# Two selective-scan stages of a four-layer kernel: squares and a result copy on ScalarE, skip term, step bias and residual as TensorE products, softplus and gate reading PSUM

## The chip, the cores and the metric

The kernel runs on one core of a Trainium2 chip. The metric is device time in microseconds (us). The kernel before took 7786.44 us, the median of three runs (7783.06 to 7791.43).

## The reference, cut to what matters

Four layers run one after the other, each `x = x + s * silu(g)`, where `s` comes from a sequence mixer and `g` from a second network, both on the layer-normed `x`. Batch 8, 512 positions, width 128, fp32. The mixers of layers 0 and 2 are selective scans (L0a and L2a in the names of the kernel); the change touches these two alone. Per batch one of them computes:

```python
u, res = split(norm(x) @ in_proj_w)      # 256 + 256 columns
u = silu(causal_conv(u, conv_w, 4 taps) + conv_b)
dt, B, C = split(u @ x_proj_w)           # 8, 16 and 16 columns
delta = softplus(dt @ dt_proj_w + dt_proj_b)
h_t = exp(delta_t * A) * h_{t-1} + (delta_t * u_t) * B_t   # 256 x 16 states
y_t = sum over states of h_t * C_t
y = (y + u * D) * silu(res)
out = y @ out_proj_w                     # layer 2: + norm(x)
```

Layer 0 normalises by the root of the mean square, layer 2 by mean and variance.

## The kernel before

`mamba_net` (line 2070) is called twice, with `center=False, residual=False` for L0a and `center=True, residual=True` for L2a. The 256 inner channels are two halves `d` of 128 partitions; the free dimension holds the 512 positions of a batch. There are 16 states `n`, so 32 pairs (n, d) a batch. For each pair GpSimd forms `dbu = du * B` (L2255), ScalarE the decay `da = exp(A * delta)` in one of four PSUM banks (L2339), VectorE the scan (L2387) and, for three pairs of four, the product `hc` with C (L2396); the fourth is GpSimd's (L2260). TensorE sums the states by adding identity times `hc` into `y_ps[:, d]` (L2475).

Each engine has its own program, and `sequences` writes its order out by hand: `both(b, par)` runs through the 16 states of batch b. The end of batch b-1 (`gated`, then `result`) stands behind state 0, `result` behind state 0 on TensorE and behind state 1 on the others, and pieces of batch b+1 (`front`: norm, turn, in, tap, silus, dbc, dt, log) stand behind the states that `after_state` names, per engine. On the queue of an engine everything waits for what stands ahead of it. The first and last batch are outside the loop; the loop's body has two batches.

What the change touches:

- L2365, L2367: VectorE squares `x` and sums the squares (L0a). L2360, L2363: its moments by bn_stats (L2a). `measured` releases GpSimd's reciprocal root (L2236 to L2242).
- L2290 to L2299: ScalarE copies the step product from PSUM to `v` with its bias, then Abs, Exp, Ln. L2372: VectorE adds `max(v, 0)`: this is softplus.
- L2400, L2404, `gated`: VectorE adds the skip term `u * D` to `y_ps` into `ty` (two instructions), then multiplies by the gate `zs` into `yz`.
- L2489: TensorE's output product writes bank 0 of `y_ps`. L2412 (L2a, adding `f`) and L2414 (L0a): VectorE reads it into `result`; `stored` then releases the store on SyncE and TensorE's first state sum of the next batch, which overwrites that bank.
- L2351: VectorE forms diagonal matrices from `cols` for the four taps; L2434 uses them as products.
- `ring`: two PSUM banks, taken in turn by turn, in, conv, gate, dbc and dt products. A product waits until the previous content of its bank is read.

## Time and profile before

| | us |
|---|---|
| median of three runs | 7786.44 |
| profiled execution | 7796.52 |
| its span | 7794.6 |
| L0a, about 28 to 613 | 585 |
| L2a, about 6240 to 6840 | 600 |

The span reaches from the first to the last instruction. In the rows, PE is TensorE's products and PEld its weight loads, DVE is VectorE, ACT ScalarE, POOL GpSimd. A product of fp32 operands is two PE records, so "x4" in a timeline is two products. `[3.12 <-DVE x L2414]` says that the engine stood idle 3.12 us before the row and that VectorE's instruction of line 2414 released it. PEclk is the granted clock, 1.00 for 2.4 GHz and 0.50 for 1.2 GHz.

### The profile page before, as it was taken

What the parts mean: (1) busy time and instruction counts of PE and PEld (TensorE: products, weight loads), DVE (VectorE), ACT (ScalarE), POOL (GpSimd) and SP (SyncE); (2) the same over time, 40 slices, a digit from 0 to 9 for tenths busy, and PEclk for the clock granted to TensorE, in tenths of its full rate; (3) what the DMA queues carried; (4) which work ended last, traced back from release to release, by engine and by line L of the source; (5) the groups of instructions that cost most, each with busy time, mean ns of one, the idle gap of its engine ahead of it and who ended that gap; (6) DMA issues with size and microseconds to landing.
All of it is one profiled execution on the core that took longest, in us unless ns stands there. A gap on an engine that the chain in (4) does not pass through costs nothing. (4 is left out here: it accounts for less than half of the span.)

```text
span 7794.6 us, 241834 instructions
## 1 busy us (share of the span) xinstructions
PE 6366.5 (82%) x93078; PEld 4343.4 (56%) x93078; DVE 5662.3 (73%) x11712; ACT 4278.5 (55%) x7973; POOL 4672.3 (60%) x3762
## 2 busy tenths in 40 slices
PE   5776999999999999999998599977888757734268
PEld 2333666666666666666665588874555423322256
DVE  6885888888887888888886477766777668853533
ACT  5553666666666666666665344436777655512012
POOL 5776777777777777777776254544444357723000
PEclk8888999999999999999999799999999978867579
DMA  3332112112112112112111200001110033333001
GB/s 116 123 135 57 50 47 66 47 51 64 48 51 60 51 47 63 50 50 61 50 51 39 70 6 6 6 20 27 23 31 23 17 134 126 132 121 87 10 14 33
DMA packets 344463, 440.90 MB, mean 57 GB/s; under 512 B 151976, under 2 KB 235648, under 8 KB 324416
## 3 DMA queue, kind: packets, MB, share of 16 engines
q1 hardware_dynamic: 335632, 405.19, 17.0%
q8 instruction: 759, 12.44, 0.7%
q10 hardware_dynamic: 1584, 15.21, 0.5%
q0 software_dynamic: 6144, 5.25, 0.4%
q14 instruction: 344, 2.82, 0.1%
HBM read 217.42 MB, written 42.14 MB: 33 GB/s over the span
## 5 line engine op out<-in xcount | busy, mean ns | idle before, releaser
L1110 PE MATMUL L0f_ring<-L0f_wqkv,L0f_hT 128*128 128x512 f32 x2324 | 1196.5, 624 | 20.5 <-issue 18.0
L849 POOL TENSOR_TENSOR L0f_qr<-L0f_qs,L0f_table 128x512 f32<-128x512 f32 x776 | 990.8, 1277 | 216.7 <-issue 115.1
L856 POOL TENSOR_TENSOR L0f_qr<-L0f_qr,L0f_m 128x512 f32<-128x512 f32 x776 | 989.3, 1275 | 138.0 <-issue 119.6
L862 POOL TENSOR_TENSOR L0f_qr<-L0f_qr,L0f_rn 128x1024 f32<-128x1024 f32 x388 | 752.0, 1959 | 422.3 <-DVE L0f_rn L1016 400.3
L890 ACT ACTIVATE L0f_qs<-L0f_ring 128x512 f32<-128x512 f32 x776 | 460.1, 593 | 625.0 <-PE L0f_ring L1110 618.1
L993 DVE TENSOR_TENSOR L0f_m<-L0f_ring,L0f_table 128x512 f32<-128x512 f32 x776 | 531.4, 685 | 46.2 <-ACT L0f_qs L890 14.5
L1001 DVE TENSOR_REDUCE L0f_ssq<-L0f_sq 128x8 f32<-128x512 f32 x776 | 528.1, 681 | 29.6 <-ACT L0f_sq L895 13.7
L1110 PEld LDWEIGHTS L0f_ring<-L0f_wqkv,L0f_hT 128*128 128x128 f32 x2324 | 382.1, 190 | 266.9 <-issue 210.5
L895 ACT ACTIVATE L0f_sq<-L0f_qs 128x512 f32<-128x512 f32 x776 | 492.0, 634 | 36.0 <-DVE L0f_ssq L1001 4.2
L1116 PEld LDWEIGHTS L0f_ring<-const_ident,L0f_qr 128*128 128x128 f32 x3088 | 361.8, 141 | 178.2 <-issue 170.5
L1116 PE MATMUL L0f_ring<-const_ident,L0f_qr 128*128 128x128 f32 x3088 | 428.2, 274 | 16.6 <-POOL L0f_qr L862 16.6
L1022 DVE TENSOR_REDUCE L0f_mx<-L0f_scores 128x8 f32<-128x512 f32 x384 | 265.6, 692 | 165.5 <-PE L0f_scores L1135 160.5
L1182 PE MATMUL L0f_ring<-L0f_wo,L0f_oT 128*128 128x128 f32 x3088 | 382.5, 277 | 2.9 <-issue 2.1
L2475 PE MATMUL L0a_y<-L0a_hc,const_ident 128*128 128x512 f32 x512 | 288.6, 698 | 108.3 <-DVE L0a_hc L2396 86.7
L1165 PEld LDWEIGHTS L0f_scores<-L0f_vmix,L0f_pT 64*32 64x32 f32 x18480 | 264.7, 105 | 190.8 <-issue 185.0
L1182 PEld LDWEIGHTS L0f_ring<-L0f_wo,L0f_oT 128*128 128x128 f32 x3088 | 362.2, 193 | 10.0 <-issue 3.6
L1135 PE MATMUL L0f_scores<-L0f_kT,L0f_qT 64*32 64x64 f32 x24576 | 337.3, 224 | 36.9 <-issue 36.9
L2475 PE MATMUL L2a_y<-L2a_hc,const_ident 128*128 128x512 f32 x512 | 283.5, 687 | 101.3 <-DVE L2a_hc L2396 85.1
L904 ACT ACTIVATE L0f_vb<-L0f_ring 128x512 f32<-128x512 f32 x386 | 230.5, 597 | 246.7 <-PE L0f_ring L1110 246.4
L2255 POOL TENSOR_TENSOR L0a_dbu<-L0a_du,L0a_bc_all 128x512 f32<-128x512 f32 x256 | 325.3, 1304 | 57.1 <-DVE L0a_du L2375 50.2
L2255 POOL TENSOR_TENSOR L2a_dbu<-L2a_du,L2a_bc_all 128x512 f32<-128x512 f32 x256 | 325.3, 1304 | 54.6 <-DVE L2a_du L2375 50.7
L1165 PE MATMUL L0f_scores<-L0f_vmix,L0f_pT 64*32 64x64 f32 x18480 | 324.2, 224 | 34.4 <-SPq L155 10.3
(533 smaller groups left out, 17157.9 us busy)
## 6 DMA issues: line engine op xcount, KB each, us to landing
L0f_vmix<-L0f_vb SPq DMA_DIRECT2D x768, 128.0 KB
L0a_bc_all<-L0a_bc_rows SPq DMA_DIRECT2D x32, 2048.0 KB, 11.2
L2a_bc_all<-L2a_bc_rows SPq DMA_DIRECT2D x32, 2048.0 KB, 11.0
L0f_vmix<-L0f_vb SPq DMA_DIRECT2D x672, 64.0 KB
L1f_vmix<-L1f_vb SPq DMA_DIRECT2D x96, 128.0 KB, 2.3
L0f_wqkv<-L_ffn_wqkv_dram SPq DMA_DIRECT2D x7, 1536.0 KB, 6.0
L2f_parts<-L2f_zero ACTq DMA_DIRECT2D x8, 1088.0 KB, 12.7
n_s<-mixer_out SPq DMA_DIRECT2D x32, 256.0 KB, 4.9
```

The source lines that it names most:

```text
L849: e.tensor_tensor(rotated, qs[:, q % QN], spread(cos, 1, 8), ALU.mult).then_inc(cosed.sem, 1)
L856: e.tensor_tensor(rotated, rotated, m2[:, q % SN], ALU.add).then_inc(added.sem, 1)
L862: e.tensor_tensor(rotated, rotated, spread(rn[:, tt, 2 * c:2 * c + 2], 3, DH), ALU.mult).then_inc(scaled.sem, 1)
L895: e.activation(sq[:, q % SN], qs[:, q % QN], ACT.Square).then_inc(squared.sem, 1)
L993: e.tensor_tensor(m2[:, q % SN].rearrange("p h (a d) -> p h a d", a=2), swapped, spread(sin, 1, 8).rearrange("p h (a d) -> p h a d", a=2), ...
L1001: e.tensor_reduce(ssq[:, tt % 2, slot(step)], sq[:, q % SN], AX.X, ALU.add).then_inc(summed.sem, 1)
L1110: e.matmul(bank[:], hT[:, buffer_of(it, step), tt * P:tt * P + P], wqkv[:, layer % 2, col:col + 512], start=True, stop=True).then_inc(full, 1)
L1116: a = e.transpose(bank[:, j * P:j * P + P], qr[:, tt % 2, 2 * c + "qk".index(what), 2 * j:2 * j + 2, :], g.ident[:])
L1165: a = e.matmul(o_ps[cols, s, h, j], pT[half, s, j, cols], values, start=True, stop=True)
L1182: a = e.matmul(bank[:, 0:C], oT[:, tt % 2, j, :], wo[:, j, :], start=j == 0, stop=j == pairs - 1)
L2255: e.tensor_tensor(dbu[:, s], du[:, par, d], bc_all[:, n // QN, 0, n % QN], ALU.mult).then_inc(dbu_ready.sem, 1)
L2475: e.matmul(y_ps[:, d], g.ident[:], hc[:, (2 * n + d) % 4], start=n == 0, stop=n == states - 1).then_inc(added.sem, 1)
```

## The change

The squares of L0a become a step `moment` on ScalarE, behind state 0, with an accumulator output; in L2a the moments stay on VectorE. The diagonals of the bias and of `D` join those of the taps (14 in place of 8). TensorE adds the bias as diagonal times ones ahead of each step product, the skip term as diagonal times `uc` ahead of state 0's sum, and in L2a the residual as identity times `f` ahead of the output product. ScalarE takes Abs straight from PSUM, VectorE's softplus and gate read PSUM; `v` and `ty` are gone. ScalarE copies the result, behind state 1. The diff, cut to its core:

```diff
         # gpsimd, ahead of zeroed
+            e.memset(ones[:], 1.0)
+            e.memset(mv[:, :, 0], 0.0)
         # scalar, front (moment=0)
+                if kind == "moment":
+                    if not center:
+                        for tt in range(TT):
+                            o = e.activation(sq[:, tt], g.f[...], ACT.Square,
+                                             scale=C ** -0.5, accum_out=mv[:, tt, 1:2])
+                        o.then_inc(measured.sem, 1)
+                    return
         # scalar, front dt
-                        e.activation(v[:, d], ring.at(step)[:], ACT.Identity,
-                                     bias=cols[:, d, taps + 1:taps + 2]).then_inc(ring.empty_of(step), 1)
-                    e.drain()
-                    e.activation(ln1[:], v[:], ACT.Abs)
+                        e.activation(ln1[:, d], ring.at(step)[:], ACT.Abs)
         # scalar, back
+                if kind == "result":
+                    e.wait_ge(*out_full(b, "o"))
+                    e.wait_ge(sent[par], (b - par) * 8 + 16)
+                    e.activation(result[:, par], y_ps[:, 0].rearrange("p (t c) -> p t c", t=TT), ACT.Copy).then_inc(stored.sem, 1)
         # vector
-                for k in range(taps):
+                for k in range(taps + 3):
                     e.tensor_scalar(taps_of[:, d, k], g.ident[:], cols[:, d, k:k + 1], None, ALU.mult)
-                        e.scalar_tensor_tensor(sq[:], x, 1.0 / C, x, ALU.mult, ALU.mult)
-                        e.drain()
-                        e.tensor_reduce(mv[:, :, 1], sq[:], AX.X, ALU.add)
-                        e.scalar_tensor_tensor(delta[:, par, d], v[:, d], 0.0, ln1[:, d], ALU.max, ALU.add)
+                        e.scalar_tensor_tensor(delta[:, par, d], ring.at(step)[:], 0.0, ln1[:, d], ALU.max,
+                                               ALU.add).then_inc(ring.empty_of(step), 1)
-                    for d in range(D2):
-                        e.scalar_tensor_tensor(ty[:, d], uc[:, par, d], cols[:, d, taps + 2:taps + 3], y_ps[:, d],
-                                               ALU.mult, ALU.add)
-                    e.drain()
-                    e.tensor_tensor(yz[:], ty[:], zs[:, par], ALU.mult).then_inc(yz_ready.sem, 1)
-                elif kind == "result":
...
+                    e.tensor_tensor(yz[:], y_ps[:], zs[:, par], ALU.mult).then_inc(yz_ready.sem, 1)
         # tensor: dt, state 0, result
+                        e.matmul(ring.at(step)[:], taps_of[:, d, taps + 1], ones[:], start=True, stop=False)
+                    if n == 0:
+                        e.matmul(y_ps[:, d], taps_of[:, d, taps + 2], uc[:, par, d], start=True, stop=False)
+                        if residual:
+                            e.matmul(y_ps[:, 0, tt * C:tt * C + C], g.ident[:], g.f[...], start=True, stop=False)
```

## Rows read from the trace of the kernel before

**Rows 1.** Busy time by stretch, the two scan stages: length, then each engine, PEclk, DMA share, GB/s

```profile
28.00:613.00 585.00, 429.07 (x928) 181.82 (x928) 476.06 (x537) 298.31 (x434) 417.59 (x359) 0.85 0.30 120
6240.00:6840.00 600.00, 423.95 (x928) 179.58 (x928) 489.54 (x665) 312.02 (x465) 430.69 (x387) 0.82 0.32 126
```

**Rows 2.** Timeline of VectorE, first stage: start, length, engine, line, operation

```profile
142.96 1.41 DVE L2400 SCALAR_TENSOR_TENSOR L0a_ty<-L0a_uc,L0a_cols,L0a_y 128x512 f32<-128x512 f32 x2 [0.45 <-PE L0a_y L2475]
...
144.44 1.23 DVE L2404 TENSOR_TENSOR L0a_yz<-L0a_ty,L0a_zs 128x1024 f32<-128x1024 f32 x1
...
145.58 1.76 DVE L2365 SCALAR_TENSOR_TENSOR L0a_sq<-f 128x512 f32 x1
...
148.36 2.35 DVE L2387 TENSOR_TENSOR_SCAN L0a_da<-L0a_da,L0a_dbu 128x512 f32<-128x512 f32 x2 [0.26 <-issue]
...
151.80 0.68 DVE L2414 COPY L0a_result<-L0a_y 128x512 f32<-128x512 f32 x1
...
184.61 2.35 DVE L2387 TENSOR_TENSOR_SCAN L0a_da<-L0a_da,L0a_dbu 128x512 f32<-128x512 f32 x2 [3.03 <-ACT L0a_da L2339]
```

**Rows 3.** Timeline of TensorE's products, first stage

```profile
145.72 3.78 PE L2489 MATMUL L0a_y<-L0a_w_out,L0a_yz 128*128 128x128 f32 x16 [2.80 <-DVE L0a_yz L2404]
...
152.62 8.28 PE L2475 MATMUL L0a_y<-L0a_hc,const_ident 128*128 128x512 f32 x12 [3.12 <-DVE L0a_result L2414]
...
178.34 1.88 PE L2475 MATMUL L0a_y<-L0a_hc,const_ident 128*128 128x512 f32 x4
...
180.06 1.88 PE L2442 MATMUL L0a_ring<-L0a_xnT,L0a_w_in 128*128 128x512 f32 x4
...
427.47 7.08 PE L2475 MATMUL L0a_y<-L0a_hc,const_ident 128*128 128x512 f32 x12 [3.12 <-DVE L0a_result L2414]
...
559.82 9.49 PE L2475 MATMUL L0a_y<-L0a_hc,const_ident 128*128 128x512 f32 x16 [0.87 <-DVE L0a_result L2414]
```

**Rows 4.** Busy time by stretch around the boundaries, for the granted clock (PEclk)

```profile
152.60:158.50 5.90, 5.88 (x7) 2.51 (x8) 5.38 (x6) 2.89 (x7) 2.15 (x3) 0.50 0.14 44
559.80:564.65 4.85, 4.83 (x6) 2.17 (x7) 4.80 (x5) 1.30 (x2) 0.99 (x1) 0.50 0.18 54
6786.69:6790.56 3.87, 3.87 (x5) 1.80 (x6) 3.82 (x4) 0.99 (x2) 0.04 (x1) 0.50 0.23 72
424.80:427.40 2.60, 0.00 (x0) 0.00 (x0) 2.60 (x5) 1.23 (x2) 2.46 (x3) 1.00 0.00 0
428.10:431.50 3.40, 3.40 (x6) 1.34 (x5) 3.40 (x5) 2.24 (x5) 0.72 (x1) 0.50 0.24 77
```

**Rows 5.** Timeline of ScalarE, first stage

```profile
151.32 1.30 ACT L2339 ACTIVATE L0a_da<-L0a_delta,L0a_decay 128x512 f32<-128x512 f32 x2 [7.48 <-DVE L0a_hc L2396]
...
181.12 0.60 ACT L2312 ACTIVATE L0a_zs<-L0a_ring 128x512 f32<-128x512 f32 x1 [1.88 <-PE L0a_ring L2442]
...
188.50 0.69 ACT L2290 ACTIVATE L0a_v<-L0a_ring,L0a_cols 128x512 f32<-128x512 f32 x1 [1.13 <-PE L0a_ring L2450]
...
191.31 1.06 ACT L2295 ACTIVATE L0a_ln<-L0a_ln 128x1024 f32<-128x1024 f32 x1
```

**Rows 6.** Timeline of VectorE and of TensorE at a boundary of the second stage

```profile
6447.10 1.41 DVE L2400 SCALAR_TENSOR_TENSOR L2a_ty<-L2a_uc,L2a_cols,L2a_y 128x512 f32<-128x512 f32 x2 [0.45 <-PE L2a_y L2475]
6455.57 7.31 PE L2475 MATMUL L2a_y<-L2a_hc,const_ident 128*128 128x512 f32 x12 [1.92 <-DVE L2a_result L2412]
```

**Rows 7.** Groups of instructions by line (busy us, mean ns)

```profile
L2372 DVE SCALAR_TENSOR_TENSOR L0a_delta<-L0a_v,L0a_ln 128x512 f32<-128x512 f32 x16 | 15.3, 996 | 30.5 <-ACT L0a_ln L2299 30.5
L2323 ACT ACTIVATE L0a_upad<-L0a_ring 128x512 f32<-128x512 f32 x16 | 9.4, 590 | 4.8 <-PE L0a_ring L2463 4.1
L1764 ACT ACTIVATE L1f_scores<-L1f_scores,L1f_nmx,L1f_rn 128x128 f32<-128x128 f32 x504 | 218.7, 437 | 31.2 <-DVE L1f_nmx L1870 30.1
L1764 ACT ACTIVATION_READ_ACCUMULATOR L1f_scores<-L1f_scores,L1f_nmx,L1f_rn 128x1 f32 x504 | 106.0, 210 | 0.0
```

**Rows 8.** Timeline of VectorE at the start of the first stage

```profile
38.93 1.46 DVE L2351 TENSOR_SCALAR L0a_taps_of<-const_ident,L0a_cols 128x128 f32<-128x128 f32 x7
```

More of the change, by code:

```diff
@@ L2086, in mamba_net, with after_state @@
     ND_DVE = [k for k in ND if k not in ND_POOL]
-    FRONT = ([("norm",), ("turn",)] + [("in", c) for c in range(D2)] + [("tap", i) for i in range(2 * D2)] +
+    FRONT = ([("moment",), ("norm",), ("turn",)] + [("in", c) for c in range(D2)] + [("tap", i) for i in range(2 * D2)] +
              [("silus",), ("dbc",), ("dt",), ("log",)])
-    def after_state(norm, turn, silus, dbc, dt, log):
-        place = {("norm",): norm, ("turn",): turn, ("silus",): silus, ("dbc",): dbc, ("dt",): dt, ("log",): log}
+    def after_state(moment, norm, turn, silus, dbc, dt, log):
+        place = {("moment",): moment, ("norm",): norm, ("turn",): turn, ("silus",): silus, ("dbc",): dbc, ("dt",): dt, ("log",): log}
         place.update({("in", c): turn + 1 for c in range(D2)})
@@ L2115, in mamba_net @@
         upad = r.sb("upad", [P, D2, taps - 1 + SEQ])
-        taps_of = r.sb("taps_of", [P, D2, taps, P])
+        taps_of = r.sb("taps_of", [P, D2, taps + 3, P])
+        ones = r.sb("ones", [P, SEQ])
         uc = r.sb("uc", [P, 2, D2, SEQ])
@@ L2261, in back @@
                                         ALU.mult).then_inc(hc_pool_ready.sem, 1)
-            sequences(e, front, back, after_state(norm=2, turn=3, silus=7, dbc=8, dt=11, log=11))
+            sequences(e, front, back, after_state(moment=0, norm=2, turn=3, silus=7, dbc=8, dt=11, log=11))
         @block.scalar
@@ L2340, in back @@
                                  scale=decay[:, d, n:n + 1]).then_inc(da_ready.sem, 1)
-            sequences(e, front, back, after_state(norm=3, turn=5, silus=10, dbc=11, dt=12, log=13))
+            sequences(e, front, back, after_state(moment=0, norm=3, turn=5, silus=10, dbc=11, dt=12, log=13))
         @block.vector
@@ L2363, in front @@
                             e.bn_aggr(mv[:, tt], stats[:, tt])
[L2364 to L2368 removed]
+                        e.drain().then_inc(measured.sem, 1)
                 elif kind == "dt":
@@ L2449, in front @@
                         e.wait_ge(*ring.free(b, step))
+                        e.matmul(ring.at(step)[:], taps_of[:, d, taps + 1], ones[:], start=True, stop=False)
                         e.matmul(ring.at(step)[:], w_dt[:, d * P:d * P + P], dbc[0:rank, par],
-                                 start=True, stop=True).then_inc(ring.full_of(step), 1)
+                                 start=False, stop=True).then_inc(ring.full_of(step), 1)
                     return
@@ L2474, in add @@
                         e.wait_ge(*stored(b, "s", 1))
-                    e.matmul(y_ps[:, d], g.ident[:], hc[:, (2 * n + d) % 4], start=n == 0, stop=n == states - 1).then_inc(added.sem, 1)
+                    if n == 0:
+                        e.matmul(y_ps[:, d], taps_of[:, d, taps + 2], uc[:, par, d], start=True, stop=False)
+                    e.matmul(y_ps[:, d], g.ident[:], hc[:, (2 * n + d) % 4], start=False, stop=n == states - 1).then_inc(added.sem, 1)
                 if kind == "state":
@@ L2487, in back @@
                     for tt in range(TT):
+                        if residual:
+                            e.matmul(y_ps[:, 0, tt * C:tt * C + C], g.ident[:],
+                                     g.f[:, bass.ds(b * TT + tt, 1), :].rearrange("p o c -> p (o c)"), start=True, stop=False)
                         for d in range(D2):
                             o = e.matmul(y_ps[:, 0, tt * C:tt * C + C], yz[:, d, tt * P:tt * P + P], w_out[:, d, :],
-                                         start=d == 0, stop=d == D2 - 1)
+                                         start=d == 0 and not residual, stop=d == D2 - 1)
                     o.then_inc(out_full.sem, 1)
-            sequences(e, front, back, after_state(norm=0, turn=3, silus=9, dbc=10, dt=11, log=11), gated=0, result=0)
+            sequences(e, front, back, after_state(moment=0, norm=0, turn=3, silus=9, dbc=10, dt=11, log=11), gated=0, result=0)
 def ttt_net(nc, g, name, w):
```

25 lines of the change are left out of this document (7 added, 18 removed).

## The prediction, made before the changed kernel ran

> **What bounds the kernel now.** I read the busy time by stretch first, to see how much of the kernel the change can reach. The two selective-scan stages take 585 and 600 us of 7794.6; in both VectorE is the busiest engine, at 476 of 585 and 490 of 600 us, with TensorE at 429 and 424 [rows 1]. Eight batches make some 68 us each. A share of 81% is no proof of a bound, so the second view is the timelines of the boundary between two batches, engine by engine.
>
> VectorE at a boundary [rows 2]: the skip term (two instructions from 142.96), the gate product at 144.44, squares and their sum for the next batch from 145.58, the scans of state 1 at 148.36, the copy of the old batch's result at 151.80. TensorE meanwhile [rows 3]: the output product runs 145.72 to 149.50, then the engine idles 3.12 us until VectorE has read the result, because the accumulator bank is the same; the state sums start again only at 152.62, 9.66 us after the skip term began. From there TensorE has no wait left: its rows follow each other back to back into the gate products at 180.06, two of those shown [rows 3]. The first gate product is what ScalarE waited for, 1.88 us before the first gate Silu at 181.12 [rows 5], and behind ScalarE's table load VectorE stands still 3.03 us for state 11 [rows 2]. So the path of a batch runs: VectorE through the boundary, then **TensorE from its restart to the gate products**, then ScalarE. VectorE's own scans are hidden in the middle part, with 3 us to spare.
>
> The third view is the granted clock [rows 4]. TensorE comes out of the boundary at 1.2 GHz (0.50) and stays there 5.9 us after the restart at 152.6. At the last boundary, where nothing but the result read lies in the gap (0.87 us idle before 559.82 [rows 3]), it stayed slow for 4.85 us in the first stage and 3.87 in the second. Once, at 424.8, the clock was up right behind the output product and fell again at 428.1, after an idle gap like those above. I price TensorE's path as restart plus half of the slow time: 9.66 + 2.95 = 12.6 us. At the two boundaries with the loop's branch it is 11.8 (restart 10.1 after the skip term, at 427.47 [rows 3], and 3.40 us slow [rows 4]); mean of the six, 12.3. In the second stage the restart is at 8.5 (6447.10 to 6455.57 [rows 6]) with 3.9 us slow, 10.4; its six boundaries lie between 10.3 and 11.8, mean 10.7.
>
> **The change, part by part** (times count from where the skip term begins now).
>
> *Skip term to TensorE, squares to ScalarE.* VectorE loses 1.48 (142.96 to 144.44) and, in the first stage alone, 2.78 (145.58 to 148.36). The gate product now reads PSUM beside SBUF; the nearest rows are the skip instructions themselves, 1.41 us for two of 512 columns with one PSUM operand [rows 2], against 996 ns each for the delta instructions with none [rows 7], so I leave it at 1.2 us. The output product starts at 1.3 in place of 2.8. ScalarE's four squares with accumulator cost 437 + 210 ns each, overlapping [rows 7], some 1.8 us or at most 2.6, between the decays of states 0 and 1. ScalarE idles 7.48 us in that stretch (before 151.32 [rows 5]), and state 1 is not scanned until after the gate product: cost nothing. Without that cover it would be 1.8 us a batch. The second stage keeps its moments on VectorE.
>
> *Result copy to ScalarE.* VectorE loses 0.60 a batch. This adds a wait: ScalarE now stands for the output product, and the decays of state 2 are queued behind it, with VectorE's scans behind them. Output product 1.3 to 5.1 (3.78 us slow [rows 3]), copy 0.59 as other ScalarE reads of PSUM [rows 7], to 5.9; decay of state 2 at 6.6. VectorE is ready at 4.7, so it stalls 1.9. What matters is that TensorE restarts at 6.0, 3.7 earlier.
>
> *Skip matmuls.* Two 128x512 products per batch right behind the restart. Two such products (four records) start 1.72 us apart at 2.4 GHz [rows 3], so +1.72, all on TensorE's path. Slow time after the restart: the idle gap is now about 0.9, as at the last boundaries (3.87 and 4.85), with none possible as at 424.8; between 0 and 6 I take 3, costing 1.5. Path: 6.0 + 1.7 + 1.5 = 9.2, against 12.3. **First stage: 3.1 x 6 = 18.7 us.** VectorE by its own rows would finish state 3 at about 13.4 in place of 16.9, so it does not undo this.
>
> *Residual on TensorE, second stage.* Eight records on top of 16: 5.7 us in place of 3.78 if slow throughout, about 5.1 if the clock rises inside. Restart 7.3 (7.9 if slow); slow time then taken as 0, bound 6. Path: 7.3 + 1.7 = 9.0 against 10.7. **Second stage: 1.7 x 6 = 10 us.**
>
> *Step bias as product, softplus from PSUM.* TensorE +1.72 before the second step bank is full. ScalarE loses two reads (0.69 each) and a 1.06 us Abs, gains two Abs of 0.6 from PSUM. Now: first read 188.50, Exp 191.31 [rows 5]. Then: bank 0 at 189.4, bank 1 at 191.1, Abs to 191.7, Exp 191.8. ScalarE's chain to the decays of state 13, which VectorE waits for, is 0.45 late. VectorE's two delta instructions fall from 996 [rows 7] toward 0.74, with their drain some 0.6 less in all. Net 0.15 better, x14 = 2 us; bounds from -1.7 to +0.6 a batch. The banks are now held until VectorE's read at state 14; their next user is the transpose at state 3 of the next batch, so nobody waits.
>
> *Ends.* First boundary (no old result), first stage: squares go, +2; second stage -0.3. Last boundary +0.8 and +0.2. Tail: +1.5 in the first stage, the skip term before the last output product; -0.1 in the second, where the residual eats it. Front: in the first stage squares no longer queue behind the diagonal products on VectorE, +0.9; in the second six more of these products at 0.2 us [rows 8] come before the moments, -1.2; the longer step product costs 0.35 in each.
>
> Sum: 18.7 + 10 + 2 + 2 - 0.3 + 1.0 + 1.4 + 0.9 - 1.2 - 0.7 = 33.8, say **34 us**. The profiled execution took 7796.5 us (span 7794.6), 10 over the median of 7786.4, 0.13%. Against its own time this gives 7762.5; against the median, 7752.5.
>
> **The rivals.**
>
> *VectorE's saving counts in full.* If VectorE were the path throughout, 1.48 x 16, 2.78 x 7, 0.60 x 14, 0.6 x 14 and the front make 61 us: 7725. For it: its busy share is the highest in both stages, and the two thirds of a batch outside the ScalarE stalls show it without idle time. Against: TensorE without a gap from 152.62 and the 3.03 us stall that ScalarE's wait for it makes. 0.09.
>
> *The gain goes back to the slow clock.* If TensorE stays at 1.2 GHz about 6 us after every restart, as at 152.6 [rows 4], paths are 6.0 + 1.7 + 3.0 = 10.7 (gain 1.6) and 7.9 + 1.7 + 3.0 = 12.6 (loss 1.9): 10 - 11 + 5 for the rest, a gain of some 3: 7783. Half way to it lies 7768. For it: TensorE's idle time before the output product stays. Against: the shorter gap. 0.15.
>
> *TensorE becomes the bound and makes it slower.* Place: from the restart to the taps, where four more products (the skip pair and the residual's eight short records) run at half speed. The sum turns at 6.5 us of slow clock after each restart, and passes 0.2% slower at 9. At 14 us the paths are 14.7 and 16.6, 50 us worse less 5: 7831. Against: no slow stretch behind a restart in these two stages is over about 6. 0.06.
>
> *ScalarE is the wrong engine for the copy.* If it took three times VectorE's 0.68 us [rows 2], 1.45 us more at each of 14 boundaries would delay the restart, 20 us in all: 7773. Against: the same copy form on ScalarE takes 590 ns [rows 7]. 0.02. The Trainium skill (ScalarE: Activation LUTs, Rules for kernel authors) advises VectorE for plain multiplies and adds, up to about 3 times faster per element, though for bf16. By that rule the move is a loss; this trace's fp32 rows from PSUM contradict it.
>
> *The change does only half of what its words say:* squares leave VectorE in the first stage only. This is in the sum.
>
> **How the numbers follow.** My forecast has 0.68. The range goes from near the full VectorE saving, 7730, to the slow-clock case, 7784; it takes in the bounds of the step part. What a measurement of this kernel can tell from no change is about 0.2%, 15.6 us: 7771 to 7802. Faster: 0.66 of the forecast plus 0.09, 0.75. Same: 0.02 + 0.15 + 0.02, 0.19. Slower: 0.06.
>
> **What would show it.** Right: at a first-stage boundary the state sums restart about 6 us after the gate product begins, with a gap near 0.9; VectorE shows a stall of about 2 us for ScalarE before state 2; the first stage is some 24 us shorter, the second 9; the wait before the gate Silu stays between 1 and 2 us. Wrong: a slow stretch over 6 us behind the restart, no stall at state 11 (VectorE would be the path), ScalarE's copy over 0.7 us, or a table load before the squares.

## The result, and the profile after

The kernel after took 7729.36 us, the median of four runs (7710.90 to 7742.21), against 7788.93 for the kernel before, now also the median of four: ratio 0.9921, 95% interval 0.9897 to 0.9944. That is 59.6 us less where 34 had been forecast, and just below the range. The profiled execution (7710.9 us, span 7709.1) is the shortest of the four. Its span is 85.5 us shorter than that of the kernel before; its two scan stages, measured as below, account for 63 us of that, and the rest comes from stages that the change does not touch. So everything below is read from the stages, which repeat far better than the whole: the same kernel built and run once more, on another chip, gave 7729.19 us and the same batch periods within 0.05 us.

Busy time by stretch, the two stages of the kernel after (to set beside [rows 1]: length, PE, PEld, DVE, ACT, POOL, PEclk, DMA share, GB/s), and under them the six batches between the first and the seventh gate product of each:

```profile
28.00:568.00 540.00, 429.24 (x992) 175.90 (x992) 435.97 (x502) 299.75 (x498) 410.06 (x361) 0.92 0.32 130
6169.70:6752.00 582.30, 437.28 (x1056) 187.71 (x1056) 465.50 (x644) 304.18 (x465) 423.61 (x389) 0.88 0.33 129
143.16:513.37 370.21, 316.85 (x744) 132.04 (x744) 324.52 (x367) 219.90 (x358) 305.92 (x265) 0.92 0.35 141
6311.70:6695.44 383.74, 323.44 (x792) 143.07 (x792) 332.15 (x415) 213.92 (x318) 306.16 (x265) 0.91 0.34 137
```

The same six batches in the kernel before:

```profile
142.96:552.40 409.44, 318.32 (x696) 137.58 (x696) 357.66 (x397) 220.59 (x319) 312.49 (x265) 0.83 0.32 128
6379.92:6779.27 399.35, 313.54 (x696) 135.69 (x696) 351.00 (x433) 220.55 (x319) 312.93 (x265) 0.84 0.33 132
```

A batch of L0a went from 68.24 to 61.70 us and one of L2a from 66.56 to 63.96. In L0a VectorE's busy time fell by 33.1 us over six batches and its idle time by 6.1 (from 51.8 to 45.7). The granted clock rose from 0.83 to 0.92. L0a ends at 567.3 in place of 612.5 (45.2 us, of them 39.2 in the six periods), and L2a lasts 538.7 in place of 556.5 us from its first normalisation (17.8, of them 15.6 in the periods). Ahead of that first normalisation the six more diagonal matrices cost 1.25 us (from VectorE's first diagonal to ScalarE's first row of the norm 6.70 us, 5.45 before), as the forecast had it; the stages as counted here leave this out.

A boundary of L0a in the kernel after, VectorE (beside [rows 2]):

```profile
267.55 1.22 DVE L2406 TENSOR_TENSOR L0a_yz<-L0a_y,L0a_zs 128x1024 f32<-128x1024 f32 x1 [0.45 <-PE L0a_y L2470]
268.69 2.33 DVE L2393 TENSOR_TENSOR_SCAN L0a_da<-L0a_da,L0a_dbu 128x512 f32<-128x512 f32 x2
270.93 1.27 DVE L2402 TENSOR_TENSOR L0a_hc<-L0a_da,L0a_bc_all 128x512 f32<-128x512 f32 x2
272.21 1.23 DVE L2393 TENSOR_TENSOR_SCAN L0a_da<-L0a_da,L0a_dbu 128x512 f32<-128x512 f32 x1
...
302.56 2.35 DVE L2393 TENSOR_TENSOR_SCAN L0a_da<-L0a_da,L0a_dbu 128x512 f32<-128x512 f32 x2 [2.41 <-ACT L0a_da L2349]
...
311.81 2.35 DVE L2393 TENSOR_TENSOR_SCAN L0a_da<-L0a_da,L0a_dbu 128x512 f32<-128x512 f32 x2 [2.90 <-ACT L0a_da L2349]
```

and TensorE there (beside [rows 3]):

```profile
258.31 3.78 PE L2470 MATMUL L0a_y<-L0a_hc,const_ident 128*128 128x512 f32 x4 [3.04 <-DVE L0a_hc L2402]
263.73 3.78 PE L2470 MATMUL L0a_y<-L0a_hc,const_ident 128*128 128x512 f32 x4 [1.64 <-DVE L0a_hc L2402]
268.83 2.05 PE L2487 MATMUL L0a_y<-L0a_w_out,L0a_yz 128*128 128x128 f32 x16 [1.31 <-DVE L0a_yz L2406]
271.74 1.10 PE L2469 MATMUL L0a_y<-L0a_uc,L0a_taps_of 128*128 128x512 f32 x2 [0.87 <-DVE L0a_hc L2402]
```

The skip term, the squares and the result copy are gone from VectorE, and it passes from the gate product into the scans with no idle time in these rows. The gap ahead of TensorE's restart is 0.87 us, as forecast. But the restart comes 4.2 us behind the start of the gate product, not 6.0, because the output product took 2.05 us and not 3.78. The granted clock around that boundary (beside [rows 4]):

```profile
257.70:268.00 10.30, 7.57 (x8) 2.35 (x8) 9.75 (x13) 3.80 (x12) 7.62 (x7) 0.51 0.53 210
268.00:271.70 3.70, 2.05 (x16) 1.86 (x16) 3.70 (x5) 0.70 (x2) 3.50 (x4) 1.00 0.77 319
271.70:280.00 8.30, 8.26 (x23) 3.93 (x24) 8.29 (x10) 7.05 (x13) 7.31 (x8) 1.00 0.10 32
```

The slow stretch now lies under the last sums of the old batch and is over before the output product starts. Six of the seven boundaries of L0a are like this; the first is the one that was forecast (output product 3.78, restart at 5.92). In L2a five of seven restarts come at 6.6 to 7.3 us and two at 5.0 to 5.1.

### The profile page after: what moved, and what is told of

Read it like the earlier page. It is cut to its first block and busy times, and to the rows that moved or that the text cites. A ratio compares the mean times of both kernels' runs of the same rounds, so it can differ in the third digit from the quotient of the medians.

```text
span 7709.1 us, 242164 instructions
## 1 busy us (share of the span) xinstructions
PE 6363.5 (83%) x93206; PEld 4336.1 (56%) x93270; DVE 5594.9 (73%) x11658; ACT 4270.3 (55%) x8037; POOL 4655.8 (60%) x3766
## 5 line engine op out<-in xcount | busy, mean ns | idle before, releaser
L993 DVE TENSOR_TENSOR L0f_m<-L0f_ring,L0f_table 128x512 f32<-128x512 f32 x776 | 530.9, 684 | 38.9 <-POOL L0f_qr L856 10.7
L1135 PEld LDWEIGHTS L0f_scores<-L0f_kT,L0f_qT 64*32 64x32 f32 x24576 | 270.6, 105 | 122.6 <-issue 122.5
L1165 PE MATMUL L0f_scores<-L0f_vb,L0f_pT 64*32 64x64 f32 x6160 | 326.0, 225 | 0.0
```

Of the source, the lines that this page charges most:

```text
L993: e.tensor_tensor(m2[:, q % SN].rearrange("p h (a d) -> p h a d", a=2), swapped, spread(sin, 1, 8).rearrange("p h (a d) -> p h a d", a=2), ...
L1135: a = e.matmul(s_ps[rows, s, h, j], qT[half, tt % 2, GP * u + j, rows], kT[half, GP * u + j, cols], start=False, stop=j == GP - 1)
L1165: a = e.matmul(o_ps[cols, s, h, j], pT[half, s, j, cols], values, start=True, stop=True)
```

## The experiments

Periods are means of six batches, gate product to gate product, as above. "Stages" is the end of L0a plus the length of L2a from its first normalisation; its difference to the kernel before or after is what an edit is worth. The runs come from at least five chips, and the kernel before took 7783.69 to 7798.75 us (medians) beside them: ratios and stages can be compared across the table, medians only with care.

| kernel | median us | ratio to before (95%) | L0a | L2a | stages |
|---|---|---|---|---|---|
| before | 7788.93 | | 68.24 | 66.56 | 1169.0 |
| after | 7729.36 | 0.9921 (0.9897 to 0.9944) | 61.70 | 63.96 | 1106.0 |
| ctl | 7729.19 | 0.9913 (0.9896 to 0.9931) | 61.66 | 63.97 | 1105.8 |
| b_warm | 7774.49 | 0.9981 (0.9972 to 0.9991) | 67.96 | 65.28 | 1156.8 |
| a_skip | 7769.86 | 0.9974 (0.9962 to 0.9987) | 67.44 | 65.83 | 1154.0 |
| u_skip | 7757.54 | 0.9955 (0.9938 to 0.9971) | 64.93 | 64.97 | 1142.9 |
| u_copy | 7745.98 | 0.9942 (0.9925 to 0.9958) | 63.83 | 65.91 | 1130.0 |
| u_sq | 7748.71 | 0.9941 (0.9924 to 0.9958) | 64.27 | 64.53 | 1126.4 |
| u_dt | 7732.06 | 0.9927 (0.9910 to 0.9943) | 61.73 | 63.11 | 1099.6 |
| late4 | 7771.81 | 0.9973 (0.9964 to 0.9983) | 64.96 | 65.04 | 1138.0 |
| aw | 7728.43 | 0.9916 (0.9899 to 0.9934) | 60.92 | 61.98 | 1087.6 |
| aw_late4 | 7754.90 | 0.9949 (0.9933 to 0.9966) | 63.29 | 64.35 | 1123.3 |
| aw_skip | 7772.99 | 0.9970 (0.9958 to 0.9983) | 64.63 | 64.79 | 1141.0 |
| aw_sq | 7759.94 | 0.9956 (0.9940 to 0.9972) | 63.43 | 63.07 | 1113.0 |
| aw_result | 7776.23 | 0.9969 (0.9956 to 0.9981) | 64.05 | 66.12 | 1132.6 |
| pad | 7724.35 | 0.9923 (0.9907 to 0.9940) | 63.03 | 64.16 | 1113.8 |
| fold | 7710.81 | 0.9898 (0.9882 to 0.9915) | 61.62 | 61.53 | 1085.5 |
| fws | 7710.99 | 0.9889 (0.9871 to 0.9906) | 60.34 | 61.86 | 1078.2 |
| fw | 7694.60 | 0.9875 (0.9857 to 0.9893) | 59.49 | 60.47 | 1065.0 |
| fw5 | 7690.62 | 0.9877 (0.9861 to 0.9894) | 59.48 | 60.47 | 1063.0 |

Medians of so few runs scatter by some 10 us (aw and ctl, on one chip, are equal there and 18 us apart in the stages, 20 in the profiled spans), so a small edit is judged by its stages.

### b_warm: the clock kept up in the kernel before

```diff
 elif kind == "gated":
+    warm(b, 2)      # products into a bank that nobody reads
     for d in range(D2):
         add(states - 1, d)
+    warm(b, 2)
 elif kind == "result":
...
     o.then_inc(out_full.sem, 1)
+    warm(b, 1)
```

> The kernel before, with five more TensorE products per batch around the boundary (128x512, into a bank that nobody reads): two ahead of the last sums, two behind them, one behind the output product. VectorE's work is unchanged. Theory C (the clock's part in the gain is real: TensorE idle around the boundary lets the granted clock fall, and the output product and the restart pay for it): the granted clock stays at its upper level across the boundary, the output product takes about 2.05 us instead of 3.78, and the L0a period falls from 68.24 by 1.7 to 3 us, 14 boundaries give 24 to 42 us. Rival V (only VectorE's own work counts, the clock follows it): period 68.2 or a little more by the added products, time within 10 us of before or above it.

The period of L0a fell by 0.28 us and that of L2a by 1.28; the stages got 12 us shorter, half of the least that theory C had put down. The output product took 2.05 us at three of the first six boundaries of L0a, and yet the restart came 8.65 us behind the gate product's start at all six (8.2 or 8.6 before): there VectorE copies the result only behind the scans of state 1, so a faster output product leads to nothing.

The clock was not kept up where it would have counted. Its mean over the six batches of L0a was 0.92, but over the four microseconds behind each restart it read 0.50 to 0.62, as in the kernel before (0.50 to 0.58). So L0a of this run doesn't tell what the clock behind the restart is worth. L2a does, for there it differed from batch to batch. One restart of L0a (218.98) and two of L2a, with the clock in the third number from the end:

```profile
218.98:222.98 4.00, 4.00 (x5) 1.82 (x6) 3.94 (x5) 2.69 (x6) 0.24 (x2) 0.50 0.21 66
6373.49:6377.49 4.00, 3.99 (x10) 1.85 (x11) 4.00 (x5) 2.86 (x7) 1.99 (x3) 1.00 0.21 66
6437.67:6441.67 4.00, 4.00 (x6) 1.81 (x7) 3.95 (x5) 2.69 (x6) 0.61 (x2) 0.64 0.21 68
```

All six restarts came 7.45 us behind the gate product. The four batches with the clock at 0.97 to 1.00 behind it took 64.17 to 64.27 us, the two at 0.64 and 0.57 took 65.3 and 65.5 (without the stall at the loop's turn, 1.9 to 2.2 us in two of the six, which the section on pad is about). A slow stretch behind the restart costs 1.2 us a batch here, whether the output product was fast (2.05 at 6430.23) or slow (3.58 at 6561.90). This is the second term of the forecast's path.

### a_skip, u_skip, u_copy, u_sq, u_dt: one part alone, and the parts undone

a_skip is the kernel before with the skip term on TensorE; the others are the kernel after with one part put back as it was (the diffs are the parts of the change, reversed).

> The kernel before with the skip term alone moved to TensorE. VectorE's two instructions of 0.64 us, a drain and 0.45 us of the gate product go (1.7 to 1.8 us per batch). Theory V: L0a period 68.24 to 66.4, L2a 66.56 to 64.7, 25 us in all. Theory P: the skip pair costs TensorE as much as its earlier restart brings: 0 to 8 us in all. The removal from the kernel after cost 3.2 us per period in L0a and 1.0 in L2a, so the parts need not add up; a value over 2.5 us in L0a would say that a wait for ScalarE or GpSimd goes with it.

> The kernel after with the skip term put back on VectorE (two instructions of about 0.64 us ahead of the gate product and a drain) and the two skip products taken off TensorE. Theory V: the period of L0a grows from 61.70 by VectorE's 1.3 to 1.5 us, 14 boundaries give 18 to 21 us. Theory C: the gate product ends 1.3 us later, the idle ahead of the output product grows, the clock is still low there (3.78 us in place of 2.05), and the period grows by 3 to 4 us, 40 to 55 us in all. The forecast's own reckoning (TensorE's path, the skip pair costing it 1.7): about nothing, -5 to +5 us.

> The kernel after with the copy of the result back on VectorE (0.68 us per batch), residual still on TensorE. Theory V: +0.7 us per period, +10 us in all. Theory C: +0.7, and as the clock was already up before the output product, no more than that. Forecast's reckoning (TensorE waits for the copy on either engine, VectorE then late behind it): 0 to +3 us.

> The kernel after with the squares and their sum put back on VectorE (L0a alone; 1.76 us and a reduction, and two drains) at the place they had before. Theory V: the period of L0a rises by the 2.3 to 3 us that they take, 16 to 22 us in all, L2a unchanged (63.96). Theory P: TensorE has caught up by then or not; under 1 us per period, 0 to 7 us in all.

> The kernel after with the step's part undone: no bias products, ScalarE writes v with the bias and takes the absolute value from it, VectorE's delta reads v and ln1 from its memory (2.00 us for two in place of 1.28). Theory: the bias products lengthen VectorE's wait behind state 13 (2.90 us, 2.02 before) and the shorter delta gives 0.7 back, so the sum is +0.2 per batch for the change: undone, -3 us in all, within 5 us of after. Forecast: undone +2 us. Rival: the two bias products (2 x 1.0 us) also push the sums behind them and cost over 1 us per batch: undone, -14 us or more.

The prices do not add up at first sight. In L0a the skip term is worth 0.80 us a period when it alone is moved (15 us in the stages, between what the two theories had), and 3.23 when it is taken out of the finished change. The copy holds 0.69 us of VectorE and costs 2.13; squares 2.57; the step part 0.03 in L0a and -0.85 in L2a, where undoing it gains. Undone, skip, copy and squares make 7.9 of a total of 6.5.

Most of the surplus is one thing counted three times. u_skip, u_copy and u_sq each have two stalls in L0a, 1.92 to 2.07 us where VectorE's loop turns back, 0.66 us a period; the kernel after has none, and a_skip has them as the kernel before has (the section on pad is about them). Without the stalls the three make 5.9 us, and the whole change is worth 5.85. In L2a the stall accounts for the 0.57 us by which u_sq moved a stage that it does not touch (1.93 and 1.90, 0.64 a period), and 1.0 of the 1.95 us of u_copy (3.04 and 3.05 us).

That a part undone costs more than its own work is seen in the rows of u_skip, VectorE at one of its boundaries:

```profile
402.87 1.40 DVE L2407 SCALAR_TENSOR_TENSOR L0a_ty<-L0a_uc,L0a_cols,L0a_y 128x512 f32<-128x512 f32 x2
404.35 1.68 DVE L2411 TENSOR_TENSOR L0a_yz<-L0a_ty,L0a_zs 128x1024 f32<-128x1024 f32 x1
...
410.92 1.23 DVE L2394 TENSOR_TENSOR_SCAN L0a_da<-L0a_da,L0a_dbu 128x512 f32<-128x512 f32 x1 [1.46 <-ACT L0a_da L2350]
```

Beside its own 1.7 us (with the gate product longer by 0.45) and the stall, the skip term brings back a wait of 1.46 us ahead of state 2 (6.7 us over five batches): the output product is slow again (3.50 us there), ScalarE stands for it, and the decay of state 2 stands behind ScalarE's copy. This is the stall that the forecast had at 1.9 us in every batch. In the kernel after it is missing from six of seven boundaries of L0a. The granted clock behind the restart also fell again, to 0.50 to 0.55 at five of the seven boundaries of L0a in u_skip and to 0.50 at two in u_sq, so the price of one part holds some of the clock's as well.

The price of the step part has to be read from like boundaries, for u_dt has three slow output products in the six batches of either stage where the kernel after has one in L0a and five in L2a. Behind a fast one its batches take 60.7 to 61.1 us in L0a (61.4 to 61.5 after) and 62.2 in L2a (62.4 after). So the step part of the change costs some 0.5 us a batch in L0a and 0.2 in L2a; most of the 0.85, and the 0.03 too, is where the slow boundaries fell.

### late4: TensorE's restart made as late as the forecast had it

```diff
     o.then_inc(out_full.sem, 1)
+    warm(b, 4)
```

> The kernel after with four more TensorE products (128x512, into a bank nobody reads) behind the output product of each batch, so that the state sums restart some 2.6 us later (4 x 0.86, less the 0.87 gap that they fill). That makes the path of TensorE in a batch as long as the forecast took it to be (about 9 us instead of 6). Theory P (the forecast's way of reckoning is right and only its clock term was wrong): the period of L0a rises from 61.70 to about 64.5 to 65, VectorE waits 3 us per batch for a sum, 35 to 45 us in all. Theory V (VectorE's own work and its waits for ScalarE set the period, TensorE's lag has slack): period under 62.7, under 15 us in all.

L0a came to 64.96 us, 3.26 more than after. Theory P's number was 64.5 to 65. L2a, with a restart at 7.6 us at all but its first boundary, came to 65.04 (63.96 after), and the stages grew by 32 us, under P's 35 to 45. VectorE at one boundary:

```profile
338.37 1.21 DVE L2406 TENSOR_TENSOR L0a_yz<-L0a_y,L0a_zs 128x1024 f32<-128x1024 f32 x1
...
344.56 1.23 DVE L2393 TENSOR_TENSOR_SCAN L0a_da<-L0a_da,L0a_dbu 128x512 f32<-128x512 f32 x1 [1.55 <-ACT L0a_da L2349]
...
348.57 0.69 DVE L2402 TENSOR_TENSOR L0a_hc<-L0a_da,L0a_bc_all 128x512 f32<-128x512 f32 x1 [1.67 <-PE L0a_y L2478]
```

No work was added to VectorE, and it is 3.2 us later, by one wait for ScalarE and one for a sum. So the kernel after is not simply bound by VectorE's own work: a TensorE that restarts at 8.2 us takes half of the gain of L0a back.

### aw, fw: the clock kept up in the kernels after and fold

```diff
+def still(k):
+    for _ in range(k):
+        e.matmul(y_ps[:, 0], zeros[:], w_in[:], start=False, stop=False)
...
+    if n == states - 1:
+        still(2)
     if n:
         for d in range(D2):
             add(n - 1, d)
 elif kind == "gated":
+    still(2)
     for d in range(D2):
         add(states - 1, d)
+    warm(b, 1)
```

> The kernel after with five products per batch (128x512) that change nothing, in TensorE's own gaps around the boundary: two with a weight of zeros ahead of the sums of state 14, two ahead of those of state 15, one into an idle bank behind the last sums. Theory C2 (VectorE's wait of about 1.4 us for ScalarE ahead of state 2, and the last of its waits for sums, come and go with the granted clock during the output product): the clock stays at its upper level across the boundary, the output product takes 2.05 us in L0a and the pair of residual and output about 2.6 in L2a in every batch; L0a, where six of seven boundaries had that already, stays at 61.7; L2a, where five of seven were slow, falls from 63.96 by about 1.3 to 62.7; 9 us in all. Theory V2 (the clock plays no part): no change, or slower by what the added products delay.

> The kernel with the folded bias and the same five products. There the boundaries of L0a were slow (output product 3.78 us, VectorE's wait of 1.5 us ahead of state 2 in each). Theory C2: that wait goes, the period of L0a falls from 61.62 to about 60.2 and that of L2a from 61.53 to about 61.0; 12 to 15 us below the folded kernel, 7697. Theory V2: within 3 us of the folded kernel or above it.

> The kernel after once more, unchanged, to see how far its periods and its time vary from one build and run to the next. Both theories: 7729 within 0.2%, L0a period 61.7, L2a 64.0, each within 0.6 (the kernel with the squares put back moved L2a, which it does not touch, by 0.57).

With these five products the clock reads 1.00 over the six batches of either stage, and the restart comes at 4.1 to 4.2 us (L0a) and 5.1 to 5.2 us (L2a) in every batch. L2a fell by 1.99 us a period, more than expected, and L0a by 0.75; 18 us in the stages. In fold the same products gave 2.13 in L0a and 1.06 in L2a. Not all of the gain in L0a is the output product's: five of the six batches of L0a had that at 2.05 us in the kernel after already, and still went from 61.4 or 61.5 us to 60.9 or 61.0. The same is seen inside one kernel. VectorE in L2a of ctl, two boundaries in a row, and the gate product behind them:

```profile
6463.91 1.23 DVE L2406 TENSOR_TENSOR L2a_yz<-L2a_y,L2a_zs 128x1024 f32<-128x1024 f32 x1 [0.45 <-PE L2a_y L2470]
...
6471.65 1.23 DVE L2393 TENSOR_TENSOR_SCAN L2a_da<-L2a_da,L2a_dbu 128x512 f32<-128x512 f32 x1 [1.50 <-ACT L2a_da L2349]
...
6528.24 1.22 DVE L2406 TENSOR_TENSOR L2a_yz<-L2a_y,L2a_zs 128x1024 f32<-128x1024 f32 x1
...
6534.40 1.22 DVE L2393 TENSOR_TENSOR_SCAN L2a_da<-L2a_da,L2a_dbu 128x512 f32<-128x512 f32 x1
...
6590.64 1.23 DVE L2406 TENSOR_TENSOR L2a_yz<-L2a_y,L2a_zs 128x1024 f32<-128x1024 f32 x1 [0.45 <-PE L2a_y L2470]
```

and the clock over residual and output product at each:

```profile
6465.20:6471.20 6.00, 5.05 (x25) 4.89 (x25) 4.62 (x12) 0.76 (x2) 5.55 (x8) 0.62 0.32 134
6529.60:6533.30 3.70, 2.94 (x24) 2.75 (x24) 3.37 (x11) 0.70 (x2) 3.26 (x6) 1.00 0.60 252
```

The batch behind the slow boundary takes 64.33 us (6463.91 to 6528.24), the one behind the fast 62.40. The wait of 1.50 us ahead of state 2 is most of the difference.

### aw_skip, aw_sq, aw_result, aw_late4: the same parts on top of aw

> The kernel aw (after, with five idle products that keep the clock up across the boundary) with the skip term back on VectorE. Its removal from VectorE is worth, by its instructions, 2 x 0.64 us, a drain, and up to 0.45 us of the gate product: 1.3 to 1.8. Theory (full count and the clock apart): L0a period 60.92 to 62.3 to 62.7, L2a 61.98 to 63.4 to 63.8; the rest of the 3.23 that it cost in the kernel after was the clock's. Rival (the skip term itself costs over 2.5, by TensorE's later restart): 63.9 or more.

> The kernel aw with the squares and their sum back on VectorE, L0a alone. Theory: full count, 2.3 to 2.6 us, L0a 60.92 to 63.3, L2a unchanged at 61.98 within 0.05 (in the kernel after it had moved by 0.57 with the clock's phase). Rival: the cost is in waits for GpSimd, whose reciprocal root comes later, and exceeds 3.

> The kernel aw with the result step as it was before: on VectorE, with the residual added there in L2a and the residual products gone. Theory: VectorE's 0.68 us in L0a and about 0.7 in L2a counts in full, and the restart of the sums moves from 4.2 to about 5.4 us behind the gate product, since VectorE copies behind its scans; L0a +0.7 to +1.5, L2a +0.3 to +1.0 (0.6 us of residual products go). Rival: nothing, the copy is off the path on either engine.

> The kernel aw with four more idle products behind the output product: the sums restart 2.6 us later, with the clock up and ScalarE's copy on time. Theory: VectorE's wait ahead of state 2 for ScalarE stays away, and only its wait for sums shows: L0a 60.92 to between 61.5 and 62.5 (late4, with the slow output product too, came to 64.96). Rival: most of late4's 3.26 us was the sums' lag itself: 63.5 or more.

Only aw_late4 and aw_sq keep the clock up nearly throughout (0.98 to 1.00 over six batches; 0.95 to 0.97 in the other two). aw_late4 settles TensorE's part: with the output product at 2.05 us and ScalarE's copy on time, a restart 2.45 us later (6.6 in place of 4.15) costs 2.37 us a period, between what the two sides had put down. TensorE's path counts nearly one for one, from a restart at about 4 us on.

The other three did not give the pure price of VectorE's work. aw_skip cost 3.71 in L0a, over its 1.7: its output product takes 2.6 to 3.6 us in spite of the idle products, so 1.1 us of the wait ahead of state 2 is back, and 0.7 is the stall at the loop's turn. aw_result cost 3.13 and 4.14; the restart moves to 5.4 and 6.97 us, as VectorE copies behind its scans, the clock behind it reads 0.57 to 0.68 at ten of the twelve restarts, and VectorE then waits for sums. aw_sq cost 2.51 us in L0a and also 1.09 in L2a, which it does not touch. All three show the stall, which neither after nor aw has (aw_sq and aw_result in both stages); the next run is about it. It is 0.65 us a period of aw_sq in either stage, so that the 2.51 hit the number expected by luck; the rest of the 1.09 lies behind two slow output products (3.98 and 4.24 us).

The batches of aw_sq without the stall do give a pure price, that of the squares. From 463.70 to 526.45 the clock is 1.00 and the restart 4.1 us behind the gate product, as in aw, and the batch takes 62.75 us, 1.88 over the 60.87 in aw. VectorE is 2.5 us later at the scans of state 1; 0.6 of this is taken off its wait for ScalarE at state 11 (1.79 for 2.40). TensorE, without idle time between restart and gate products in aw, now waits twice for VectorE:

```profile
473.75 1.98 PE L2485 MATMUL L0a_y<-L0a_hc,const_ident 128*128 128x512 f32 x4 [0.56 <-DVE L0a_hc L2405]
476.58 1.98 PE L2485 MATMUL L0a_y<-L0a_hc,const_ident 128*128 128x512 f32 x4 [0.41 <-DVE L0a_hc L2405]
```

So with the clock up the two engines are nearly level: TensorE's path counts from the first microsecond, VectorE's behind some 0.6 us.

### pad: code added, no work

```diff
 i = 2 * n + d
+if (n, d) in ((11, 0), (13, 0)):
+    for _ in range(6):
+        e.sem_inc(passed, 1)
 e.wait_ge(*da_ready(b, (n, d)))
```

> The kernel after with twelve semaphore increments per batch added on VectorE, in front of its waits for ScalarE at states 11 and 13, where it stands still for 2.4 and 2.9 us anyway. No work is added. 
The stall came back in both stages, at the two boundaries where the loop turns back. VectorE in pad, and below it POOL:

```profile
266.18 1.23 DVE L2396 TENSOR_TENSOR_SCAN L0a_da<-L0a_da,L0a_dbu 128x512 f32<-128x512 f32 x1 [2.01 <-POOL L0a_dbu L2256]
```

```profile
260.99 4.94 POOL L2256 TENSOR_TENSOR L0a_dbu<-L0a_du,L0a_bc_all 128x512 f32<-128x512 f32 x4 [2.07 <-DVE L0a_du L2381]
```

The profile names POOL, but the operand that this first scan needs is the first of those four (about 1.24 us each) and was there near 262.2, four microseconds before. The operand is not what VectorE waits for; the DMA queues point to its own code. The row of the queues for instruction fetches (packets, MB, share) over six batches of L0a, in the kernel before, after, and in pad:

```profile
q14 instruction: 18, 0.15, 0.1%
```

```profile
q14 instruction: 8, 0.07, 0.0%
```

```profile
q14 instruction: 18, 0.15, 0.1%
```

The kernel before has the same stall, 2.21 and 1.94 us in L0a and 1.93 and 1.90 in L2a, 8 us in all; the kernel after has none. The fetches also stand at the right time. In the kernel before, in the three microseconds that end with the first stalled scan (275.0 to 278.0), the queue shows

```profile
q14 instruction: 1, 0.01, 1.2%
```

and there is a packet likewise ahead of its second stall (411.5 to 414.5) and that of pad (263.2 to 266.2), and none at the same place in the kernel after (261.5 to 264.5). L0a of pad ended 6.6 us later, not 4: three more boundaries fell into the slow clock, with a wait of 1.4 us each ahead of state 2. In the whole time the difference is within the scatter.

### fold: the step bias without products

```diff
-e.activation(ln1[:, d], ring.at(step)[:], ACT.Abs)
+e.activation(ln1[:, d], ring.at(step)[:], ACT.Abs, bias=cols[:, d, taps + 1:taps + 2])
...
-e.activation(ln1[:], ln1[:], ACT.Ln, bias=1.0).then_inc(logged.sem, 1)
+for d in range(D2):
+    o = e.activation(ln1[:, d], ln1[:, d], ACT.Ln, bias=eb[:, d], scale=eb[:, d])   # eb = exp(bias)
+o.then_inc(logged.sem, 1)
...
-e.scalar_tensor_tensor(delta[:, par, d], ring.at(step)[:], 0.0, ln1[:, d], ALU.max,
+e.scalar_tensor_tensor(delta[:, par, d], ring.at(step)[:], nb[:, d], ln1[:, d], ALU.max,   # nb = -bias
...
-e.matmul(ring.at(step)[:], taps_of[:, d, taps + 1], ones[:], start=True, stop=False)
```

> The kernel after with the step bias folded into ScalarE's and VectorE's instructions in place of the bias products: the absolute value takes the bias as its operand, the logarithm takes exp(bias) as scale and as addend (so it yields log(1+e)+bias, two instructions of 128x512 in place of one of 128x1024), and delta is max(v, -bias) plus that. VectorE keeps the short delta (1.28 us), TensorE loses the two bias products. Putting the whole step part back saved 0.9 us per L2a batch and nothing in L0a; the fold should give both: the wait behind state 13 falls from 2.90 to about 2.0, one more instruction on ScalarE costs 0.2 us in the wait behind state 14. Expected: L0a 61.0, L2a 63.1, 8 to 14 us below the kernel after. Rival: the waits for ScalarE only shift to the next state, within 4 us of it.

Its stages are 20.5 us shorter than those of the kernel after, more than the 8 to 14 expected: L0a stayed at 61.62 (61.0 expected), L2a fell to 61.53 (63.1 expected). By the ratios (0.9898 and 0.9921) it is some 18 us faster, though the intervals overlap. VectorE in L0a of fold:

```profile
385.23 1.23 DVE L2411 TENSOR_TENSOR L0a_yz<-L0a_y,L0a_zs 128x1024 f32<-128x1024 f32 x1 [0.46 <-PE L0a_y L2474]
...
391.62 1.23 DVE L2398 TENSOR_TENSOR_SCAN L0a_da<-L0a_da,L0a_dbu 128x512 f32<-128x512 f32 x1 [1.75 <-ACT L0a_da L2354]
...
421.98 2.35 DVE L2398 TENSOR_TENSOR_SCAN L0a_da<-L0a_da,L0a_dbu 128x512 f32<-128x512 f32 x2 [2.41 <-ACT L0a_da L2354]
...
429.20 2.35 DVE L2398 TENSOR_TENSOR_SCAN L0a_da<-L0a_da,L0a_dbu 128x512 f32<-128x512 f32 x2 [0.88 <-ACT L0a_da L2354]
...
434.70 1.23 DVE L2398 TENSOR_TENSOR_SCAN L0a_da<-L0a_da,L0a_dbu 128x512 f32<-128x512 f32 x1 [1.97 <-ACT L0a_da L2354]
```

The wait behind state 13 fell from 2.90 to 0.88 and the next rose from 1.51 to 1.97. In L0a all of it was hidden, because the boundaries there turned slow and the wait ahead of state 2 (1.75 us here) took its place. The idle products of fw took that wait away again. fw and fw5 (the same kernel, built again) are the fastest: 7694.60 and 7690.62 us, 35 us below the kernel after by fw and ctl, which ran on one chip, and 41 and 43 in the stages; the intervals of both are just clear of that of ctl.

> The kernel fw once more, unchanged, with five rounds. Expected 7694 within 0.15%, ratio to before 0.9875.

### fws: ScalarE's four Silus parted

> The kernel of the run before this one with ScalarE's four Silus behind state 10 parted: the two of the convolution stay, the two of the gate go behind state 11. VectorE's wait of 2.4 us for ScalarE there should halve; if ScalarE only hands the wait to the next state (which is followed by the copy of the rank and B/C rows), the wait moves and the sum of the two stays. Expected 60.2 to 59.5 in L0a, 7 us; the rival 0, and slower if the later rows delay the broadcasts that the next batch waits for.

The rival held, and worse: the wait of 2.4 us behind state 10 went, one of 3.4 came behind state 11 (17.2 us over five batches), and the period rose by 0.85 and 1.39 us. I take it that the chain from the x projection to the step was delayed more than the split saved; no run parts the two.

## Why the prediction was wrong

The direction, both stages as the place of the gain, and the way of reckoning held. What failed is one step, **"Skip matmuls"** with the restart that it takes from the step before: "Path: 6.0 + 1.7 + 1.5 = 9.2, against 12.3".

- *Output product "3.78 us slow".* In L0a it took 2.05 in six of seven boundaries, so the restart came at 4.2 and not 6.0.
- *"Slow time after the restart ... between 0 and 6 I take 3, costing 1.5."* There was none: over the four microseconds behind each of the 14 restarts of both stages the clock reads 1.00. It comes back before or during the output product, where before it came back behind the restart.

With both terms as measured (the mean restart of the six batches is 4.4 us, the first boundary at 5.92 included) the path is 4.4 + 1.7 = 6.1, and 12.3 - 6.1 is 6.2 us. In L2a the restart at a mean of 6.7 gives 8.4, so 10.7 - 8.4 = 2.3, with "slow time then taken as 0" right.

- *What the forecast did not have:* the stall where VectorE's loop turns back, 8 us in the two stages, 0.69 and 0.64 us a period. It was in the trace of before, under POOL's name, ahead of the skip term, from which the forecast's path counts; so it stood in no term, and it comes on top. Path and stall together make 6.9 and 2.9 us, against 6.54 and 2.60 measured: the reckoning is 0.3 us a batch too high in both stages.

The runs support both terms. A restart 2.45 us later cost 2.37 (aw_late4), and a slow stretch behind the restart 1.2 us a batch (L2a of b_warm). The forecast's price, half of its length, would have been 1.4 and 1.7 us there (an estimate, from 0.64 and 0.57 over four microseconds).

- *"so it stalls 1.9"*, ahead of state 2, was right where the output product was slow (1.75 at the first boundary of L0a, 1.50 at 6471.65 in ctl) and void where it was fast.
- *Residual on TensorE*: in ctl, products of residual and output from 6465.29 to 6470.3, 5.0 us at a mostly slow boundary, forecast 5.1. Right.
- *Squares*, "cost nothing": right. They take 294 + 187 ns each, below the 437 + 210 taken, in ScalarE's idle time.
- *Result copy* "0.59": 597 ns, so the fourth rival fell; the Trainium skill's preference for VectorE in plain arithmetic (ScalarE: Activation LUTs, Rules for kernel authors; it names adds and multiplies, not copies) does not show in a copy of 128x512 fp32 from PSUM, which VectorE does in 0.68.
- *Step part*, "Net 0.15 better": delta fell by 0.7 (679 ns each), more than the 0.6, but VectorE's wait behind state 13 grew by 0.9, not 0.45. ScalarE's rows show why: its two reads of the step banks now wait 1.98 and 1.57 us for TensorE, each behind a bias product. Between like boundaries the sum is a loss of 0.5 us a batch in L0a and 0.2 in L2a (u_dt); the forecast's lower bound, -1.7, holds.
- *The first rival*, "VectorE's saving counts in full", gave 61 us and came nearest: VectorE's busy time fell by 5.5 us a batch of L0a (3.1 in L2a), and its idle time fell by 1.0 (it grew by 0.5 in L2a), of which 0.7 is the stall. But its reason is only half of the truth. late4 and aw_late4 add nothing to VectorE and lose 3.3 and 2.4 us. VectorE's saving could count nearly in full because TensorE's path had shrunk by as much; that the two came out so close was luck, not something that the rival had worked out.
- *The second and third rivals* rested on a slow stretch behind every restart; there was none in the kernel after.

ScalarE's rows in the kernel after, at the step:

```profile
307.31 0.60 ACT L2299 ACTIVATE L0a_ln<-L0a_ring 128x512 f32<-128x512 f32 x1 [1.98 <-PE L0a_ring L2443]
309.47 0.60 ACT L2299 ACTIVATE L0a_ln<-L0a_ring 128x512 f32<-128x512 f32 x1 [1.57 <-PE L0a_ring L2443]
310.14 1.06 ACT L2301 ACTIVATE L0a_ln<-L0a_ln 128x1024 f32<-128x1024 f32 x1
```

**Still open:** why the slow stretch begins ahead of the sums of state 14 in L0a of the kernel after and some two microseconds later against the boundary in fold or L2a. The idle gaps of TensorE are alike (3.04 and 3.50 us), and edits as small as pad's changed which boundaries were slow. Also open is the pure price of the skip term and of the copy, since no run that undid them left the clock and the code's place alone, and what makes up the 0.3 us a batch by which the reckoning is too high.

## What to carry to other kernels

Where a wait ends on TensorE, price each product at both clocks before adding: here the output product and the sums behind the restart, both taken at the slow level, were worth, by the reckoning above, 3.1 of the 6.5 us that a batch of the first stage gained, and a few idle products in gaps that exist anyway made the fast level certain. Read the clock where the work is that counts, not its mean over the stage: 0.92 hid a slow stretch behind every restart of b_warm's first stage. When work leaves an engine, look at the engine that follows it in the chain as well, for a saving counts in full only if both shrink. And a part undone from a finished change is not the part's own price: waits and stalls come and go with it, so compare batches that differ in nothing else.

## What the runs showed of the hardware that was not expected

- VectorE stood still where its loop turned back, 1.9 to 2.2 us (3.0 in the second stage of u_copy), with an instruction fetch in the DMA queues at that moment (18 against 8 packets in six batches), and twelve semaphore increments a batch brought this on. The profile puts it down to GpSimd, or to no engine.
- Whether a boundary's products run at 1.2 or 2.4 GHz repeats from build to build of one kernel (ctl has the pattern of after at all 14 boundaries) but changes with edits far from it: aw_sq edits nothing that L2a runs, and two of six output products there were slow (3.98 and 4.24 us) that in aw took 2.62.
- Products with a weight of zeros, added to an accumulation that is under way, kept the clock at 1.00 over whole stages (aw, fw) and cost nothing that shows. The same products did not hold it where VectorE had more to do ahead of the output product (aw_skip, 0.95 in L0a) or copied the result itself (aw_result, 0.97).
- The clock's level behind the restart does not follow the output product's: in L2a of b_warm a product of 2.05 us was followed by 0.64, one of 3.58 us by 1.00.
